# A gated linear-attention layer on one core: another order for the first 45 microseconds

## The reference

```python
xn = layernorm(x)                                  # x: 4 x 512 x 512
# attention branch, on xn seen as 2 x 1024 tokens, 16 heads of 128
qkv = silu(xn @ w_qkv.T); q, k, v = split(qkv)     # w_qkv: 6144 x 512
# linear attention with a decay per head, in blocks:
o_inter = (qi * q_decay) @ kv
o_intra = ((qi @ ki.T) * diag_decay) @ vi
kv      = block_decay * kv + (ki * k_decay).T @ vi
out = norm_w * rmsnorm(o)
s   = (sigmoid(xn @ w_gate.T) * out) @ w_out.T
# router branch: softmax over 64 experts, the best 8, their biases
f   = xn * sum(topk_w) + topk_w @ expert_bias[topk_idx]
y   = x + s * silu(f)
```

## Time and profile before

| what | value |
|---|---|
| median of 3 runs | 1077.23 us (1074.14 to 1080.42) |
| profiled execution | 1076.92 us |
| its span | 1075.2 us |
| mean granted TensorE clock, as a share of full speed | 0.993 |
| busy: PE, DVE, ACT, POOL | 97%, 59%, 56%, 63% |

### The profile page before, as it was taken

One profiled execution on the slowest core, in us unless ns is written; L12 is line 12 of the kernel. 1 busy time (PEld: TensorE's weight loads), 2 busy tenths in 40 slices (PEclk: granted clock), 3 DMA queues, 4 the chain that ended last, 5 costly groups with the idle time before them and its releaser, 6 DMA issues.

```text
span 1075.2 us, 15318 instructions
## 1 busy us (share of the span) xinstructions
PE 1045.3 (97%) x5540; PEld 889.4 (83%) x5540; DVE 632.7 (59%) x1047; ACT 600.5 (56%) x1074; POOL 672.2 (63%) x700
## 2 busy tenths in 40 slices
PE   7899999999999999999899989999999999999997
PEld 6688887888888887888788878888888888888886
DVE  5357556664756665556355565756666575555557
ACT  7666556564656655575455445646556465645543
POOL 6966556574766857586566775755657375665613
PEclk8999999999999999999999999999999999999999
DMA  4233223252434435345733652321334251332235
GB/s 152 77 82 83 52 63 93 67 148 70 128 98 128 122 102 154 94 108 145 283 101 94 186 162 47 86 64 46 94 97 121 67 159 48 74 94 59 63 94 183
DMA packets 214508, 112.59 MB, mean 105 GB/s; under 512 B 175520, under 2 KB 189984, under 8 KB 214432
## 3 DMA queue, kind: packets, MB, share of 16 engines
q1 hardware_dynamic: 198880, 59.68, 23.5%
q10 hardware_dynamic: 15552, 51.93, 15.1%
HBM read 66.47 MB, written 15.73 MB: 76 GB/s over the span
## 4 chain that ended last, share of the span: by engine, by line
PE 85%; DMA 4%; POOL 3%; ACT 3%; DVE 2%; SPq 1%; issue 1%; ACTq 0%; DVEq 0%; POOLq 0%
PE BS L162 7%; PE BS L164 7%; PE BS L163 7%; PE PX L162 5%; PE PX L163 5%; PE PX L164 5%; PE PS L643 5%; PE BD L162 5%; PE PO L728 5%; PE BA L162 5%; PE BD L164 5%; PE BA L164 5%; PE BD L163 5%; PE BA L163 5%; PE PT L692 4%; PE PO L712 4%
## 5 line engine op out<-in xcount | busy, mean ns | idle before, releaser
L480 POOL TENSOR_TENSOR WL<-ST,WH 128x768 fp32r<-128x768 f32 (+1 forms) x128 | 172.5, 1349 | 131.4 <-ACT WH L476 131.2
L480 POOL TENSOR_TENSOR WL<-STG,WH 128x512 fp32r<-128x512 f32 (+1 forms) x128 | 133.2, 1041 | 139.6 <-ACT WH L476 139.6
L162 PE MATMUL BS<-XH,WH 128*128 128x512 f32 x384 | 159.2, 415 | 3.1 <-ACT K L560 1.6
L164 PE MATMUL BS<-XH,WL 128*128 128x512 f32 x384 | 150.7, 392 | 0.0
L163 PE MATMUL BS<-XL,WH 128*128 128x512 f32 x384 | 150.0, 391 | 0.0
L793 DVE TENSOR_TENSOR Y<-Y,PX 128x512 f32<-128x512 f32 x104 | 71.4, 687 | 122.5 <-PE PX L164 122.0
L162 PE MATMUL BD<-XH,WH 128*128 128x512 f32 x256 | 104.2, 407 | 5.5 <-DVE K L551 5.3
L751 POOL TENSOR_TENSOR SS<-SS,SQ 128x512 f32<-128x512 f32 x60 | 86.6, 1444 | 31.7 <-ACT SQ L743 31.7
L162 PE MATMUL BA<-XH,WH 128*128 128x512 f32 x256 | 102.9, 402 | 0.0
L164 PE MATMUL BD<-XH,WL 128*128 128x512 f32 x256 | 100.7, 393 | 0.0
L163 PE MATMUL BD<-XL,WH 128*128 128x512 f32 x256 | 100.4, 392 | 0.0
(11 more groups left out here) (303 smaller groups left out, 2405.8 us busy)
## 6 DMA issues: line engine op xcount, KB each, us to landing
STG<-in_wp ACTq DMA_DIRECT2D x77, 512.0 KB, 3.8
V<-VB SPq DMA_DIRECT2D x248, 64.0 KB, 2.4
KN<-P SPq DMA_DIRECT2D x240, 48.0 KB, 2.1
XR<-in_x SPq DMA_DIRECT2D x38, 256.0 KB, 3.2
dgd<-XR ACTq DMA_DIRECT2D x16, 256.0 KB, 2.8
dxh<-WT SPq DMA_DIRECT2D x8, 448.0 KB, 3.4
dxl<-XR SPq DMA_DIRECT2D x8, 448.0 KB, 4.3
XH<-dxh ACTq DMA_DIRECT2D x7, 512.0 KB, 6.0
```

Source lines behind the costliest of these rows:

```text
L162: eng.matmul(o, ah, bh, start=first, stop=False, skip_group_check=skip)
L164: return eng.matmul(o, al, bh, start=False, stop=last, skip_group_check=skip)
L480: a = op("pool", lambda e, dst=dst, src=src: e.tensor_tensor(WL[:, u, dst], src, f32(WH[:, u, dst]), ALU.subtract))
```

## The change

It changes the calls of the beginning, and with them the order on all five engines; no product, sum or tile is added or left out.

- `EARLY` goes from 8 to 6 heads. The mask of these heads moves from the beginning into slot 6 of the loop, and the two later places get five heads each instead of four.
- The loads of the second batch on SyncE now come behind the first weight load instead of ahead of it.
- The statistics of tiles 2 and 3 of the first batch come ahead of all four norms; the weight sums of group 0 come right behind these statistics.
- `first_a` goes through the tiles in the order 0, 3, 1, 2. Piece 0 of the weights comes behind the first two norms of the second batch, piece 1 behind tile 0's splitting.
- Tile 2's differences go to `BS[0]` (before `BS[1]`), tile 3's to `BS[1]` (before PX). Their `first_blocks` come earlier. `BS[0]` is cleared behind tile 2's low parts, `BS[1]` behind product 2.
- Products 1, 2 and 5 stood behind tile 1's mixing, behind tile 3, and behind product 2. Now product 1 stands behind tile 2, and 5 and then 2 behind tile 3.
- L417 of tile 1 goes from GpSimd to VectorE.

```diff
-EARLY = 8
+EARLY = 6
@@ first_low
-            en = "pool" if t < 3 else "dve"
+            en = ("pool", "dve")[t % 2]
@@ decays of the later heads
-                    lo, hi = (EARLY, 12) if b == 0 else (12, NH)
+                    lo, hi = (EARLY, 11) if b == 0 else (11, NH)
...
+        plan(6, decays_masked, 0, EARLY)
@@ the beginning
         small_load()
+        w_load(0, "sp")
         t1 = [x_tile(1, t) for t in range(4)]
-        for n in range(3):
-            w_load(n, "sp")
+        w_load(1, "sp")
+        w_load(2, "sp")
...
         first_stats(0, (0, 1), t0)
+        first_stats(0, (2, 3), t0)
+        w_sums(0)
         for t in range(4):
             n = first_norm0(t, t0[t])
             d0.append(first_turn(t0[t], banks0[t], n, tk["warm"]))
-            if t == 0:
-                first_stats(0, (2, 3), t0)
-        decays_masked(0, EARLY)
-        clear(0, tk["zero"])
         keep_warm()
         first_stats(1, (0, 1), t1)
-        w_sums(0)
-        for t in range(4):
+        for t in (0, 3, 1, 2):
             first_a(t, banks0[t], d0[t])
         first_a_low(0, PS)
+        first_stats(1, (2, 3), t1)
         first_a_low(3, PX)
-        first_stats(1, (2, 3), t1)
         first_a_low(1, PT)
         first_a_low(2, PO)
+        first_norm1((0, 1), t1)
         w_parts(0, (0,))
-        first_norm1((0, 1), t1)
-        w_parts(0, (1,))
         first_norm1((2, 3), t1)
-        pairs = ((BD, BS[1]), (PS, PX), (PT, BS[1]), (PO, PX))
+        pairs = ((BD, BS[1]), (PS, PX), (PT, BS[0]), (PO, BS[1]))
         first_blocks(0, t0, t1, *pairs[0])
         first_blocks(1, t0, t1, *pairs[1], tk["xa", 0, 0], tk["xa", 0, 3])
+        first_blocks(2, t0, t1, *pairs[2], tk["xa", 0, 1])
         first_mix(0, *pairs[0])
         first_low(0, *pairs[0])
+        w_parts(0, (1,))
         first_mix(1, *pairs[1])
-        product(0, 1)
         first_low(1, *pairs[1])
-        first_blocks(2, t0, t1, *pairs[2], tk["xa", 0, 1], tk["xm0", 0])
-        first_blocks(3, t0, t1, *pairs[3], tk["xa", 0, 2], tk["xm0", 1])
+        first_blocks(3, t0, t1, *pairs[3], tk["xa", 0, 2], tk["xm0", 0])
         first_mix(2, *pairs[2])
         first_low(2, *pairs[2])
+        clear(0, tk["xm0", 2])
+        product(0, 1)
         first_mix(3, *pairs[3])
         first_low(3, *pairs[3])
-        clear(1, tk["xm0", 2])
+        product(0, 5)
         product(0, 2)
-        product(0, 5)
+        clear(1, tk["xm0", 3])
         w_parts(0, (2, 3))
```

## The result

The changed kernel took 1086.23 us (median of five runs, 1083.70 to 1090.08), the kernel before 1077.25 beside it: a ratio of 1.0083, with a 95% interval of 1.0064 to 1.0103. It is slower, by 9.0 us, and 0.23 above the range. The profiled execution is that of 1086.23 us (span 1084.4), 9.31 more than the profiled one of before.

The account below looks back on a forecast made before the run. It took the chain of waits, mostly GpSimd's, up to TensorE's lasting run at 45.51 as the bound. Terms -0.2 + 2.2 + 1.4 + 0.45 - 0.2 + 0.6 = 4.2 us later gave 1081.4; range 1078.3 to 1086.0.

Parts of the forecast that it names:

- The front: Start up to tile 0's difference blocks: near 16.0 instead of 16.75, a gain of 0.7, bounds 1.0 either side.
- Tiles 0 to 2: Splitting of the first tiles: GpSimd's lead of 2.7 us shrinks to 0.2 at tile 2's L414 near 27.2.
- The stall and the products: Product 1's seed delays tile 3's copies by 2.0; products 5, 2 and the clear follow, product 6 3.6 later.
- The clock: Rival: TensorE's clock falls to 1.2 GHz after its idle gap before 27.7; 1082 to 1086, chance 0.34.
- far price: Clock stays low also through products 5 and 2 and the clear: 2.8 more, 1085.8.
- near price: Clock low over the clear and product 1 only: 1.6 more, 5.8 in all, or 1083.
- What costs nothing: Moved mask, at most 1.1 among GpSimd's later weight parts, and a fifth exponential in two later places: taken as nothing.
- the clock's case: The forecast's outcomes with TensorE's clock falling in the beginning: 1082 to 1086, chance 0.34.
- signs of being wrong: First 256-column L480 starting before 33, or the run after 45 losing or gaining more than the shift.
- The ports: Rival: the front's norms do not wait for the sums; up to 1.8 earlier there, 1080.4, within the forecast's range.
- GpSimd's lead: Rival: its 2.7 earlier mixing start carries through to L480, at 29.1 instead of 31.77; 1074.5, chance 0.08.

Follow-up runs that it names:

- e11_order_2_5: The changed kernel with product 2 ahead of product 5 and the clear behind both: 1084.45 us, ratio 1.0058.
- e8_after_again: The changed kernel, unaltered, measured a second time: 1088.10 us, ratio 1.0099.
- e1_fill: The changed kernel with 14 and 8 matmuls of zeros, 128 columns, in TensorE's two idle stretches of the beginning: 1086.83 us, ratio 1.0083.
- e13_same_count: The changed kernel with seven of eight first warming matmuls taken out and 10 and 5 put into TensorE's two idle stretches: 1084.25 us, ratio 1.0069.
- e2_seed_late: The changed kernel with product 1's seed copy L536 behind tile 3's copies on ScalarE: 1083.39 us, ratio 1.0048.
- e5_mask: The changed kernel with eight heads' exponentials in the beginning again and their mask behind tile 3's mixing: 1085.22 us, ratio 1.0069.
- five filled kernels: Five variants of the changed kernel with matmuls of zeros in TensorE's two idle stretches of the beginning: medians from 1084.25 to 1086.83 us.
- e6: The changed kernel with TensorE's two idle stretches filled by matmuls of zeros and the mask back as well: 1086.79 us, ratio 1.0090.
- e10: The changed kernel with 22 matmuls of zeros, 64 columns, added behind the eight warming ones, filling no idle stretch: 1091.92 us, ratio 1.0124.
- e14: The kernel before with 22 matmuls of zeros, 64 columns, added behind the warming ones: 1081.24 us, ratio 1.0032.

## Why the prediction was wrong

**The front: right, in part by luck.** Blocks of tile 0 at 16.0, tile 0's mixing at 18.27 (18.2), as forecast. Two terms under it were not. The statistics of tiles 2 and 3 waited for their load until 6.28, not 5.4, so the norms began at 7.93 instead of 7.1; and the four norms took 2.94 instead of 3.8. The two errors cancel: 10.87 (10.9). Other executions of the same front had tile 0's blocks at 15.22 (`e11_order_2_5`) and 15.58 (`e8_after_again`). Two norms ran ahead of the sums and took 0.54 each, the two beside them 0.94 and 0.95. Of the sums that overlap these two, the first took 0.72 and the next two 0.90 (L458) and 0.91; the last, alone, took 0.73. So both engines pay, as the Trainium skill (SBUF — State Buffer, "Who interferes with whom") has it for their shared ports, where of two instructions that need them the second waits for the first.

**Tiles 0 to 2: right.** GpSimd's L404 at 18.77, 23.24 and 25.77 (forecast 18.7, 23.2, 25.7), tile 2's L414 at 27.24 (27.2). Of a lead of 2.7, 0.2 was left, as worked out.

**The stall and the products: right in kind, 0.8 short.** `e1_fill` has the forecast's clock and its 16.0 for tile 0's blocks. There product 6 starts at 36.10 (35.4) and the lasting run at 50.55 (49.7): +5.0 against the forecast's 4.2. Half of the missing 0.8 is the first matmul behind the clear, which takes 0.63 to the next one (28.27 to 28.90) where the sum has 0.23; in the kernel before it took the same (28.43 to 29.06). `e13_same_count` starts product 6 at 35.35 and the run at 49.81, just as forecast, but only since its front was 0.76 earlier: that match is luck.

**The clock: the step that failed.** The forecast's sum took every matmul at 0.23, with 0.58 for that; the falling clock had 0.34. The argument against it was that the gap would be shorter than the wait of 5 us at which the clock had fallen in the trace. The gap was 3.47 long, and the clock fell behind it all the same, to 0.50 from 29.1 to 39.4. That costs 3.5 up to product 6 and 3.3 of the 8.35 at the lasting run (39.59 against 36.10, 53.85 against 50.55 in `e1_fill`). The rival's far price comes near in its sum only: "through products 5, 2 and the clear" gave 4.2 + 1.6 + 2.8 = 8.6 for the start, and 8.35 came, with 0.8 too little for the order and 1.1 too much for the clock. Product 1 lost 0.8, not 1.6, since the clock fell behind the clear and the first matmul; products 5 and 2 and the clear lost 2.7. The near price (the clear and product 1 only) failed, as the clock was still low behind the second wait of 2.60; without that wait, in `e2_seed_late`, it was low to 32.5 only. The Trainium skill (TensorE: Matmul & The Clock Gate, "HAM oscillation") tells of such groups that start slow after each wait; this trace shows it at 29.1, and the repeated run shows that one of the two gaps may pass without it.

**"What costs nothing": wrong by 1.6.** The mask in slot 6 costs 0.8, since GpSimd still leads there, though TensorE's run had begun; I had seen the 1.1 and taken 0. The fifth exponential costs 0.4 in each later place: a full TensorE is no cover where ScalarE is what TensorE waits for (0.35 of idle time at 97 before). `e5_mask` takes all three steps away.

**The sum.** Of the profiled pair's 9.3: 5.0 order, 3.3 clock, 1.6 mask and exponentials, and 0.7 given back in the middle. The upper end of the range lacked the 1.6; with it, the clock's case would have reached 1087.4. One of the two signs of being wrong that were named came: the run after 45 lost these 1.6 beyond the shift.

**The other rivals.** The ports mattered. GpSimd's lead did not carry through, at the point that was named: L480 came at 40.13, behind ScalarE's eviction of product 2.

What is not shown is that the clock's 3.3 also count in the total: four of the five filled kernels are no faster than the changed kernel, and `e13_same_count` is below it, 1.0069 against 1.0083 and 1.0099, but the intervals overlap.

## What to carry to other kernels

Before work that runs beside a splitting stage is moved behind it, look at what it kept busy: the short products covered TensorE's waits, and without them the clock fell just where TensorE was the chain. A wait for which the trace has no example of the same length belongs into the sum at both clocks, and a step that is moved to a place with "a full engine" can cost about its whole duration, as the mask and the fifth exponential did here (0.8 and 0.4 each), where idle time there ends at the engine it is moved to. And matmuls of zeros that fill a gap are no free remedy: here the start came 3 us earlier and the total stayed.

## What was not expected of the hardware

- 22 matmuls of zeros added behind the first warming ones in the kernel before came with longer waits for stores near 385, 410 and 433 us (TensorE idle for 0.51, 1.34 and 2.13 instead of 0, 0.78 and 1.68) and cost 0.15 to 0.48% of the time.
- Two executions of one kernel differ in where the clock falls: after the first gap or after the second. Near 437 us, waits of 1.93 to 2.29 are followed by a lower clock in five traces (`e6`, `e8`, `e10`, `e13`, `e14`), and waits of 1.91 to 2.11 are not in three others (`e1`, `e2`, `e11`).
